# A graph network with three gather rounds: one-hots by scalar operations, two operands from PSUM

## The reference

```python
x = _layernorm(x + _L0_gnn_ref(x, ...))   # msg = (x @ W)[src] * (edge_attr @ edge_w), summed by dst, + b
x = _layernorm(x + _L1_gnn_ref(x, ...))   # msg = (x @ W_r)[src, type] * edge_weight, summed by dst, + bias, relu
x = _layernorm(x + _L2_gnn_ref(x, ...))   # h = gelu([x[src], x[dst]] @ w1 + b1); w = sigmoid(h @ w2 + b2)
                                          # normalised by degree, msg = (x @ conv_w)[src] * norm, summed by dst
x = _layernorm(x + _L3_gnn_ref(x, ...))   # 4 times: relu((x + sum of x[src] by dst) @ W1 + b1) @ W2 + b2
```

## Time and profile before

| | |
|---|---|
| median of 3 runs | 5223.94 us (5223.72 to 5233.0) |
| the profiled execution | 5221.52 us, span 5219.6 us |
| busy in the span | PE 3551.5 us, DVE 2338.9, ACT 1325.8, POOL 2503.3 |
| first gather round | 81.9 to 1354.1 us |
| second | 1412.2 to 2437.2 us |
| third | 2479.2 to 3519.4 us |

### The profile page before, as it was taken

One profiled execution on the slowest core, in us unless ns is written; L12 is line 12 of the kernel. 1 busy time (PEld: TensorE's weight loads), 2 busy tenths in 40 slices (PEclk: granted clock), 3 DMA queues, 4 the chain that ended last, 5 costly groups with the idle time before them and its releaser, 6 DMA issues. The chain is left out here.

```text
span 5219.6 us, 66479 instructions
## 1 busy us (share of the span) xinstructions
PE 3551.5 (68%) x22480; PEld 2311.7 (44%) x22480; DVE 2338.9 (45%) x5012; ACT 1325.8 (25%) x3052; POOL 2503.3 (48%) x2412
## 2 busy tenths in 40 slices
PE   3777777777676766665333333336777999999997
PEld 3444444444344544444222222226774555555554
DVE  6444444444355656554455454446773131121303
ACT  1122222222222222222334334434663010000101
POOL 3666666666477777775777777771110000000001
PEclk7888888898788888888555555557998999999998
DMA  3223333333233333332666666666776767867674
GB/s 91 83 85 104 108 96 95 109 105 99 91 91 100 93 98 102 98 103 85 170 193 186 185 189 190 186 190 217 248 245 230 305 226 302 306 232 304 221 304 156
DMA packets 509160, 863.94 MB, mean 166 GB/s; under 512 B 111675, under 2 KB 284775, under 8 KB 508868
## 3 DMA queue, kind: packets, MB, share of 16 engines
q1 hardware_dynamic: 345136, 545.24, 29.7%
q0 software_dynamic: 90496, 189.62, 14.4%
q10 hardware_dynamic: 73236, 125.49, 6.4%
HBM read 632.93 MB, written 227.18 MB: 165 GB/s over the span
## 5 line engine op out<-in xcount | busy, mean ns | idle before, releaser
L731 POOL DMA_INDIRECT big<-xw_rows,srci x784 | 804.4, 1026 | 538.0 <-DMA big<-xw_rows,srci 235.8
L1596 PE MATMUL psS<-big,xsb 128*128 128x448 f16 x2744 | 971.7, 354 | 16.3 <-issue 8.5
L1596 PE MATMUL psA<-big,xsb 128*128 128x448 f16 x2744 | 971.6, 354 | 0.0
L763 POOL DMA_INDIRECT big<-axt_rows,srci x784 | 801.5, 1022 | 264.4 <-issue 233.6
L731 POOL DMA_INDIRECT big<-ht_rows,reli x784 | 786.2, 1003 | 277.7 <-issue 229.8
L1340 PE MATMUL psS<-big 128*128 128x128 f32 x3136 | 529.7, 340 | 318.6 <-DMA big<-ht_rows,reli 314.9
L1340 PEld LDWEIGHTS psS<-big 128*128 128x128 f32 x3136 | 502.7, 252 | 403.2 <-DMA big<-ht_rows,reli 352.2
L1476 PE MATMUL ps<-identh,xsb 128*128 128x128 bf16 x784 | 101.5, 311 | 598.6 <-DVE xsb L2082 598.6
L1401 PE MATMUL ps<-xsb,attrT 128*128 128x512 f32 x392 | 287.1, 873 | 288.7 <-DVE big L1909 288.3
L796 POOL DMA_DIRECT2D x_rows<-y x12 | 11.3, 946 | 961.4 <-DVE y L2339 943.7
L2296 DVE SCALAR_TENSOR_TENSOR acc<-psS,invs,acc 128x448 f32 x56 | 38.3, 684 | 914.5 <-PE psA L1596 914.5
(11 more groups left out here) (273 smaller groups left out, 5008.7 us busy)
## 6 DMA issues: line engine op xcount, KB each, us to landing
big<-A_rows SPq DMA_DIRECT2D x112, 2744.0 KB, 13.8
A_rows<-xsb ACTq DMA_DIRECT2D x196, 416.0 KB, 2.6
xg_rows<-big SPq DMA_DIRECT2D x98, 512.0 KB, 3.9
big<-xg_rows SPq DMA_DIRECT2D x98, 512.0 KB, 3.7
marks_rows<-big SPq DMA_DIRECT2D x98, 354.0 KB
big<-marks_rows SPq DMA_DIRECT2D x98, 354.0 KB, 4.5
big<-srcq_list SPq DMA_DIRECT2D x98, 256.0 KB
ht_rows<-big ACTq DMA_DIRECT2D x28, 512.0 KB, 2.8
```

The source lines that it names most:

```text
L731: pool.indirect_dma_start(ring[g % len(ring)][:, j * D:(j + 1) * D], None, table[:, :], bass.IndirectOffsetOnAxis(ap=lists[:, g * TPG + j: ...
L763: pool.indirect_dma_start(wide[g % NS][:, j, :], None, axt_rows[:, :], bass.IndirectOffsetOnAxis(ap=srci[:, g * TPG + j:g * TPG + j + 1], ...
L1596: m = pe.matmul(sums, xs[:, t, k, :], Aring[:, r, :, t, :], start=(t == 0), stop=(t == NB - 1))
```

## The change

The comparison of a group, one DVE operation over 8 columns with two tensors as inputs (the window of `iota`, repeated, and the targets, spread), becomes eight operations over one column each, in which the target of each partition is a scalar operand. In the second round the weight is a second scalar operand of the same operation, and the separate multiplication goes, with its semaphore `r_ohraw` and the counters for it. `compare16` is cut in eight in the same way. For the third round ACT copies the last weights and the first 49 numbers of `iota` to a bank of PSUM that is free then; DVE waits for both copies once (`k_ready`) and reads them there in `dots` and `source_marks`.

```diff
+        def last_weights():
+            return ps4[:, 1024:1024 + HID]
+        def block_numbers():
+            return ps4[:, 1024 + HID:1024 + HID + NB]
...
             act.sem_inc(m_weighed, 2)
+            act.copy(last_weights(), w2r[:, :]).then_inc(k_ready, 1)
+            act.copy(block_numbers(), iota[:, 0:NB]).then_inc(k_ready, 1)
...
-            def compare(b, base, w, it):
-                return dve.tensor_tensor(tiles(onehot[:, b, :]), iota[:, window(base, w)].unsqueeze(1).broadcast_to([P, TPG, P]),
-                                         columns(dstf, it, b), ALU.is_equal)
-
-            def make_onehots(b, base, w, it, raw_count, weights):
-                if weights is None:
-                    compare(b, base, w, it).then_inc(r_oh[b], 1)
-                else:
-                    compare(b, base, w, it).then_inc(r_ohraw[b], 1)
-                    dve.wait_ge(r_ohraw[b], raw_count + 1)
-                    dve.tensor_tensor(tiles(onehot[:, b, :]), tiles(onehot[:, b, :]), columns(weights, it, b),
-                                      ALU.mult).then_inc(r_oh[b], 1)
+            def column(table, it, b, j):
+                return table[:, bass.ds(it * (2 * TPG) + b * TPG + j, 1)]
+
+            def make_onehots(b, base, w, it, weights):
+                for j in range(TPG):
+                    to, target = onehot[:, b, j * P:(j + 1) * P], column(dstf, it, b, j)
+                    if weights is None:
+                        m = dve.tensor_scalar(to, iota[:, window(base, w)], target, None, ALU.is_equal)
+                    else:
+                        m = dve.tensor_scalar(to, iota[:, window(base, w)], target, column(weights, it, b, j),
+                                              ALU.is_equal, ALU.mult)
+                m.then_inc(r_oh[b], 1)
...
-                                  iota[:, 0:NB].unsqueeze(1).broadcast_to([P, TPG, NB]),
+                                  block_numbers().unsqueeze(1).broadcast_to([P, TPG, NB]),
...
+            dve.wait_ge(k_ready, 2)
+
             def compare16(b, base, w, it):
-                dve.tensor_tensor(tiles(ohN[:, b, :]), iota[:, window(base, w)].unsqueeze(1).broadcast_to([P, TPG, P]),
-                                  columns(dstf, it, b), ALU.is_equal).then_inc(m_oh[b], 1)
+                for j in range(TPG):
+                    m = dve.tensor_scalar(ohN[:, b, j * P:(j + 1) * P], iota[:, window(base, w)], column(dstf, it, b, j),
+                                          None, ALU.is_equal)
+                m.then_inc(m_oh[b], 1)
...
-                dve.tensor_tensor(e3, e3, w2r[:, :].unsqueeze(1).broadcast_to([P, TPG, HID]), ALU.mult).then_inc(m_dot[b], 1)
+                dve.tensor_tensor(e3, e3, last_weights().unsqueeze(1).broadcast_to([P, TPG, HID]), ALU.mult).then_inc(m_dot[b], 1)
```

More of the change, by code:

```diff
@@ L264, in gnn_program @@
         s_gate = sem("s_gate")
-        r_ohraw = sem2("r_ohraw")
+        k_ready = sem("k_ready")
         r_oh = sem2("r_oh")
@@ L273, in gnn_program, with __init__ @@
         class Round:
-            def __init__(self, number, weighted, gathered, first):
+            def __init__(self, number, gathered, first):
                 self.g0 = number * NIT
-                self.w0 = weighted * NIT
                 self.gathered = gathered
@@ L283, in gnn_program @@
         r_land = [sem(f"r_land{k}") for k in range(NS)]
-        R0, R1, R2b, R3 = Round(0, 0, None, 0), Round(1, 0, None, 1), Round(2, 0, None, 0), Round(3, 0, m_gath, 0)
+        R0, R1, R2b, R3 = Round(0, None, 0), Round(1, None, 1), Round(2, None, 0), Round(3, m_gath, 0)
         USES = NG // NS
@@ L1874, in finish @@
                             with dve.Fori(1, more + 1) as w:
-                                make_onehots(b, base, w, pair, pair * nwin + w, weights)
+                                make_onehots(b, base, w, pair, weights)
                                 add_sums(b, base, w, q + w, q)
@@ L1879, in ring_round @@
                         pair = it * HALFB + n // 2
-                        make_onehots(b, load_base(pair, b), 0, pair, pair * nwin, weights)
+                        make_onehots(b, load_base(pair, b), 0, pair, weights)
                         if n0 is not None:
@@ L1902, in plain_groups @@
                     bases[g] = load_base(it, b)
-                    make_onehots(b, bases[g], 0, it, it + R.w0, weights)
+                    make_onehots(b, bases[g], 0, it, weights)
                     if n0 is not None:
@@ L1918, in round_ @@
                     q = (l * NIT + it + R.g0) * nwin
-                    qw = (it + R.w0) * nwin
                     for b in range(2):
@@ L1923, in round_ @@
                         bases.append(load_base(it, b))
-                        make_onehots(b, bases[b], 0, it, qw, weights)
+                        make_onehots(b, bases[b], 0, it, weights)
                     for b in range(2):
@@ L1928, in round_ @@
                             with dve.Fori(1, more + 1) as w:
-                                make_onehots(b, bases[b], w, it, qw + w, weights)
+                                make_onehots(b, bases[b], w, it, weights)
                                 add_sums(b, bases[b], w, q + w, q)
```

## The result

Before: 5223.83 us, median of 20 runs (5218.31 to 5233.0). With the change: 5205.23 us, median of 20 (5183.99 to 5219.86). The ratio is 0.9964, with a 95% interval of 0.9955 to 0.9973. The kernel is faster, but by 19 us where I forecast 121: the time is far outside my range of 5065 to 5146. The profiled executions spanned 5219.6 us before and 5197.2 after.

The account below looks back on a forecast made before the run. The prediction took POOL's gather issue to bound the three gather rounds; stalls of 43, 47 and 62 us, less small losses, gave gains of 31, 33 and 57, together 121 us: 5103 us, range 5065 to 5146.

Parts of the forecast that it names:

- What bounds the kernel: Three gather rounds: POOL's issue of gathers sets their length, plus a wait for landing in the first; DVE is late for nothing.
- What the stalls are worth: Three gather rounds: gathers held beyond 0.943 us lose 43, 47 and 62 us, together 152, all on the path.
- the small losses that stay: Three gather rounds: chunk normalisations 3 and 5 us in the first two; scalar-operation holds 9, 9 and 5.
- scalar operations can hold a gather for the rest of one of them: Three gather rounds: a gather over a scalar run waits up to half an operation, 0.14 us; taken as 9, 9 and 5.
- My upper end of 117 us: Three gather rounds: upper bound for holds by scalar operations, 833 gathers at 0.14 us each.
- Because today's stall ends with DVE's comparison: Gathers after the stall come at one fixed place in the run of L1851 and L1854, at another after the change.
- the gather at 417.03: First round: a gather across the end of L1851's run and the start of L1854's takes 0.95 us, losing nothing.
- Rival A: Three gather rounds: a run of scalar operations holds a gather to its end; 126 us more, 5350; chance 0.06.
- 132.03: A gather starting at 132.03 takes 3.62 us and ends at 135.65, behind the last L1854 at 135.53.
- B: Three gather rounds: each scalar operation met costs the mean half operation, 117 instead of 23 us; 5197; chance 0.08.
- C: First round: landing comes no earlier with the issue, so its 31 us gain is lost; 5134; chance 0.10.
- D: New operations take another form or gathers wait otherwise, so stalls only move; within 10 us of 5224; chance 0.03.

Follow-up runs that it names:

- e13: The changed kernel with a one-column memset behind each of the five 512-column block one-hot operations only; 5092.99 us, ratio 0.9744 against the kernel before.
- e3: The changed kernel without the ten 16-bit scalar operations of each group's block one-hots, but for one operation of one column; 5090.26 us, measured one time.
- e14: The changed kernel with its ten block one-hot operations reading their numbers from the fp32 row, not the fp16 copies; 5327.02 us, ratio 1.0189 against the kernel before.
- e11: The changed kernel with a single one-column memset between the five 512-column and the five 416-column block one-hot operations; 5143.55 us, ratio 0.9845 against the kernel before.
- e15: The changed kernel with each 512-column block one-hot operation made as four of 128 columns; 5189.27 us, ratio 0.9934 against the kernel before.

## Why the prediction was wrong

**What bounds the kernel** was right: wherever the gathers got shorter, so did the rounds, by as much.

**What the stalls are worth** (43, 47 and 62 us) was right. With the long gathers kept out (`e13`) the rounds are 1238.5, 989.4 and 983.9 us, within 3 us of the forecast each. So the small losses that stay, 12, 14 and 5 us in my sum, had the right size too. The eight operations start 0.20 us apart, as estimated, and 0.26 to 0.27 with weights; what DVE takes is hidden.

**The step that failed** is the one that reads "scalar operations can hold a gather for the rest of one of them", with its bound of half an operation and its "I take 0.09 us a group in the first two rounds, 9 us each". The form of that term was wrong, not only its size. A gather can be held to the end of the whole run of old operations, and lose 1.4 to 2.4 us. That cost 39 and 72 us in 21 and 33 gathers, where the term had 9 and 9. In the second round this is 63 of the 65 us that were missing, in the first 30 of 35; the other 5 I cannot place. My upper end of 117 us for all rounds would have held the 111 measured, but I had worked it out from many small losses and thought it far away.

**The reasoning behind it** has a claim that I made and did not follow: "Because today's stall ends with DVE's comparison, the next gathers come at one fixed place in that run; after the change they come at another." I priced the new places by a row of the old kernel, the gather at 417.03. Hundreds of unhindered gathers at one place are one sample, not hundreds. The runs show that the ten are the hold, and that the change raised its victims from 1 to 54. They do not show why: even a place that was safe 123 times of 123 before shut out 5 of 7 after, so new places, as far as windows of 0.03 us tell them apart, do not account for it.

**Rival A** had the mechanism, and put it in the wrong operations. The one row for it, 132.03, was a gather over the old ten, and I priced it over the new eight, where no row shows it. The Trainium skill (SBUF — State Buffer, Who interferes with whom) says of a DVE instruction in a two-port mode that whichever engine comes first has the shared ports for that whole instruction. For 54 gathers the traces show more, a hold over ten instructions, and for most gathers over scalar operations none at all: of 159 with both moments inside the five L1861, 35 were long, and of 112 inside the five L1864 none. By the same section a tensor_tensor with both inputs in SBUF contends with reads only. That fits the kernel before: the comparison L1817 held gathers at the early moment, while the 137 that nothing held early and that had their late moment inside it took 0.94 to 0.96 us.

**B and C** fell too. The gathers over new operations lose 0.005 and 0.017 us in the first two rounds and 0.033 in the third (98 with a mean of 0.976), not 0.14. That B's 5197 lies 8 us from the 5205 measured is chance: B adds up small losses of 833 gathers, where the kernel has large losses of 54. In `e13` the first round is 34 us shorter, so the landing came earlier with the issue. **D** is excluded by the third round and by `e3`.

## What to carry to other kernels

Where one engine's stall sets the phase of another's work, taking it away moves that work over everything that follows; price the neighbours as not yet sampled, and take the one odd row in the trace as the sample of them. An outlier ending at the end of a run of back-to-back operations means that the run, not the operation, is the hold. Then try the cheap cures first: another order of the same operations (5205 to 5094 here, nothing added), or a one-column write between them (5093).

## What the runs showed of the hardware

- The indirect DMA's issue on POOL takes 0.94 us, with 0.30 us to the next. A DVE operation with both inputs in SBUF holds it at 0.13 us after its start until that operation ends (0.47 and 0.64 us in the earlier trace rows; the 97 gathers that met L2082 so have a mean of 1.40). With one input in PSUM there was no hold: 96 gathers met L2114 at that moment and 93 L2085, and both means are 0.945. The scalar operation L2075 on 1024 bf16 columns held as well (97 gathers, mean 1.11).
- Back-to-back scalar operations of 416 or 512 columns can shut it out to the end of the run: the gather takes 2.4 to 3.4 us over ten, fp16 in; up to 4.6 us with fp32 in (`e14`). A one-column write ends the hold (1.64 us in `e11`). In runs of 128-column operations, fp32 or fp16, none of several hundred gathers was shut out (481 in `e15`, none over 1.3 us).
- Why the order of the two fives decides whether they shut gathers out (54 of them, or none), and why the ten shut out 1 gather before the change and 54 after it, stays open.
